# A pipelined attention kernel: a tail's first norm and what leads to it moved three steps ahead, beside the end of the tail before

## The reference, cut to what matters

```python
# x: (4, 1024, 256), 16 heads of 64, all float32
q, k, v = (einsum('bsd,hde->bhse', x, W) for W in (Wq, Wk, Wv))
attn = softmax(where(causal, q @ k.T / 8, -inf))
y = x + concat_heads(attn @ v) @ Wo
y = (y - mean(y)) * rsqrt(var(y) + 1e-3) * gamma + beta   # first norm
x1 = layernorm(x + y)                                     # second norm
h = silu(x1 @ wg.T) * (x1 @ wu.T)                         # hidden 768, int weights / 127
out = layernorm(x1 + h @ wd.T)                            # third norm
```

## Time and profile before

| what | value |
|---|---|
| median of three runs | 1456.25 us |
| the profiled execution, its own time | 1458.17 us |
| its span, first to last instruction | 1456.4 us |
| PE busy | 1409.0 us (97%) |
| DVE, ACT, POOL busy | 1031.7, 1002.1, 984.9 us (71, 69, 68%) |
| mean granted clock of TensorE | 0.991 |

### The profile page before, as it was taken

The page is one execution under the profiler, slowest core; times in us unless marked ns, Lnnn a source line. Parts: engine busy times, 40 slices in busy tenths (PEclk is TensorE's granted clock), DMA queues, the critical chain, the costliest instruction groups (busy, mean ns, idle before and its releaser), DMA issues.

```text
span 1456.4 us, 23825 instructions
## 1 busy us (share of the span) xinstructions
PE 1409.0 (97%) x7976; PEld 1231.7 (85%) x7976; DVE 1031.7 (71%) x2747; ACT 1002.1 (69%) x1924; POOL 984.9 (68%) x926
## 2 busy tenths in 40 slices
PE   7899999999999999999999999999999999999876
PEld 6788888888888888888888888888888888888766
DVE  7777776767676766777667676776767677677864
ACT  4777777877676676867668676676767668676534
POOL 4665666556676775867768586775867768588744
PEclk9999999999999999999999999999999999999998
DMA  3323222323342132322243122132313223121000
GB/s 130 102 81 93 62 67 95 117 52 90 103 123 73 52 95 59 110 54 58 74 117 95 52 61 72 56 120 59 95 44 110 74 60 95 51 64 55 23 12 30
DMA packets 61241, 110.46 MB, mean 76 GB/s; under 512 B 16256, under 2 KB 41600, under 8 KB 61120
## 3 DMA queue, kind: packets, MB, share of 16 engines
q1 hardware_dynamic: 61120, 108.94, 25.2%
HBM read 60.95 MB, written 13.89 MB: 51 GB/s over the span
## 4 chain that ended last, share of the span: by engine, by line
PE 73%; ACT 11%; DVE 8%; POOL 4%; issue 3%; DMA 1%; SPq 0%; ACTq 0%; POOLq 0%
PE bank L798 22%; PE bank L771 15%; PE bank L671 8%; PE bank L747 8%; PE bank L734 7%; PE bank L696 5%; PE bank L833 5%; PE bank L845 3%; ACT probs_hi L987 2%; POOL probs_lo L1428 2%; ACT probs L984 2%; ACT y_tail L1023 1%; ACT Q L967 1%; POOL h_lo L1470 1%; ACT K L967 1%
## 5 line engine op out<-in xcount | busy, mean ns | idle before, releaser
L1428 POOL TENSOR_TENSOR probs_lo<-probs,probs_hi 128x512 fp32r<-128x512 f32 x576 | 747.6, 1305 | 415.1 <-ACT probs_hi L987 412.5
L984 ACT ACTIVATE probs<-bank 128x512 f32<-128x512 f32 x576 | 344.2, 598 | 299.6 <-DVE bank L1185 217.8
L771 PE MATMUL bank<-Q,K 128*128 128x512 f32 (+3 forms) x1536 | 385.9, 353 | 3.4 <-ACT probs_hi L987 2.6
L987 ACT ACTIVATE probs_hi<-bank 128x512 fp32r<-128x512 f32 x576 | 342.2, 594 | 0.0
L771 PEld LDWEIGHTS bank<-Q,K 128*128 128x128 f32 x1536 | 252.1, 190 | 33.6 <-ACT probs_hi L987 6.2
L747 PE MATMUL bank<-K,Q 128*128 128x512 f32 (+3 forms) x768 | 245.5, 362 | 3.9 <-DMA Q<-Q 3.3
L1169 DVE CUSTOM_DVE_ANT_0 bank<-bank,mask_keys_free 128x128 f32<-128x128 f32 (+3 forms) x512 | 243.2, 506 | 4.7 <-PE bank L747 4.2
L798 PE MATMUL bank<-probs_hi,VH 128*128 128x512 f32 (+3 forms) x768 | 232.6, 343 | 7.9 <-POOL probs_lo L1428 7.2
L798 PE MATMUL bank<-probs_lo,VH 128*128 128x512 f32 (+3 forms) x768 | 234.7, 346 | 0.0
L798 PE MATMUL bank<-probs_hi,VL 128*128 128x512 f32 (+3 forms) x768 | 234.7, 346 | 0.0
L1185 DVE TENSOR_TENSOR bank<-bank,mask_queries_free 128x256 f32<-128x256 f32 (+1 forms) x320 | 119.4, 373 | 129.4 <-PE bank L771 128.9
(11 more groups left out here) (173 smaller groups left out, 2230.9 us busy)
## 6 DMA issues: line engine op xcount, KB each, us to landing
Q<-Q SPq DMA_DIRECT2D x64, 256.0 KB, 3.7
K<-K SPq DMA_DIRECT2D x64, 256.0 KB, 3.6
recip_bc<-recip_scratch SPq DMA_DIRECT2D x62, 256.0 KB, 3.4
wh<-w_scratch SPq DMA_DIRECT2D x12, 768.0 KB, 4.3
wl<-w_scratch SPq DMA_DIRECT2D x12, 768.0 KB, 5.8
wo_quad<-wo SPq DMA_DIRECT2D x16, 256.0 KB, 2.9
y<-x SPq DMA_DIRECT2D x16, 256.0 KB, 3.8
x_tail<-x SPq DMA_DIRECT2D x13, 256.0 KB, 4.4
```

Source lines behind the costliest of these rows:

```text
L771: last = mm(bk[:, at:at + cols], KX[:, n, P * i:P * i + P], QX[:, n, q0:q0 + cols], start=(KX is K1 and at == 0), stop=(KX is K2 and at + ...
L984: A(pe_[:, g % 2, :], stb[g % 2][:, :], ACT.Exp).then_inc(exp_done, 1)
L987: A(ph[:, g % RING, :], stb[g % 2][:, :], ACT.Exp).then_inc(hi_done, 1)
L1428: G.tensor_tensor(pl[:, g % RING, :], pe_[:, g % 2, :], ph[:, g % RING, :].bitcast(F32), ALU.subtract).then_inc(lo_done, 1)
```

## The change

The front of a tail, from its load to ADD, is due three steps earlier (N1, LN1R, GAM and ADD two steps earlier) for tails 0 to 10. LN2 and all that follows keep their steps, and so does the twelfth tail. Since the front now lies between the parts of the tail before, its parts count on semaphores of their own.

| part | LOAD | XB | LN1 | LN1R | N1 | GAM | ADD |
|---|---|---|---|---|---|---|---|
| engine | SP | POOL | DVE | POOL | ACT | POOL | POOL |
| step before | -5 | -1 | -1 | 0 | 1 | 2 | 3 |
| step after | -8 | -4 | -4 | -2 | -1 | 0 | 1 |

```diff
+EARLY = dict(LOAD=-8, XB=-4, LN1=-4, LN1R=-2, N1=-1, GAM=0, ADD=1)
-STEADY = tail_at(-5, -1, 7, [9, 23, 29], [13, 26, 32], 36)
-LAST_A = dict(tail_at(-5, -1, 7, [9, 18, 22], [12, 21, 25], 30), LN3=27, LN3R=28, OUT=29)
+STEADY = dict(tail_at(-5, -1, 7, [9, 23, 29], [13, 26, 32], 36), **EARLY)
+LAST_A = dict(tail_at(-5, -1, 7, [9, 18, 22], [12, 21, 25], 30), LN3=27, LN3R=28, OUT=29, **EARLY)
...
+        front_dve, front_pool = [sem(f"front_dve{g}") for g in range(2)], [sem(f"front_pool{g}") for g in range(2)]
+        front_act = [sem(f"front_act{g}") for g in range(2)]
...
-        DV = numbered(["st1a", "st1b", "mv1a", "mv1b", "st2a", "st2b", "mv2a", "mv2b", "x1lo"]
+        FRONT_DV = numbered(["st1a", "st1b", "mv1a", "mv1b"])
+        FRONT_PL = numbered(["xb", "e1", "r1", "m1", "s1", "gam", "add"])
+        FRONT_AC = numbered(["n1a", "n1b"])
+        FD, FP, FA = len(FRONT_DV), len(FRONT_PL), len(FRONT_AC)
+        DV = numbered(["st2a", "st2b", "mv2a", "mv2b", "x1lo"]
...
                 if g == 0 and tt:
-                    sp.wait_ge(tpool[0], NP * (tt - 1) + PL["add"])
+                    sp.wait_ge(front_pool[0], FP * tt)
...
             def t_ln2(n, g):
-                dve.wait_ge(tpool[g], NP * n + PL["add"])
+                dve.wait_ge(front_pool[g], FP * n + FRONT_PL["add"])
...
             def t_gamma(n, g):
-                pool.wait_ge(tact[g], NA * n + AC["n1b"])
-                G.tensor_tensor(rows_of(n, g), rows_of(n, g), over_rows(gm), ALU.mult).then_inc(tpool[g], 1)
+                pool.wait_ge(front_act[g], FA * n + FRONT_AC["n1b"])
+                G.tensor_tensor(rows_of(n, g), rows_of(n, g), over_rows(gm), ALU.mult).then_inc(front_pool[g], 1)
...
```

More of the change, by code:

```diff
@@ L311, in numbered @@
             return {k: n + 1 for n, k in enumerate(keys)}
-        DV = numbered(["st1a", "st1b", "mv1a", "mv1b", "st2a", "st2b", "mv2a", "mv2b", "x1lo"]
+        FRONT_DV = numbered(["st1a", "st1b", "mv1a", "mv1b"])
[3 more added lines that the diff above has]
+        DV = numbered(["st2a", "st2b", "mv2a", "mv2b", "x1lo"]
                       + [f"{k}{r}" for r in range(3) for k in ("tg", "hh", "h", "y2")] + ["st3a", "st3b", "mv3a", "mv3b"])
-        PL = numbered(["xb", "e1", "r1", "m1", "s1", "gam", "add", "e2", "r2", "m2", "s2", "hl0", "hl1", "hl2",
+        PL = numbered(["e2", "r2", "m2", "s2", "hl0", "hl1", "hl2",
                        "e3", "r3", "m3", "s3"])
-        AC = numbered(["n1a", "n1b", "n2a", "n2b", "x1hi", "tanh0", "tanh1", "tanh2", "n3a", "n3b"])
+        AC = numbered(["n2a", "n2b", "x1hi", "tanh0", "tanh1", "tanh2", "n3a", "n3b"])
         PEC = numbered(["tr", "g0", "u0", "d0", "g1", "u1", "d1", "g2", "u2", "d2"])
@@ L505, in tail_load @@
                 if g == 0 and tt:
-                    sp.wait_ge(tpool[0], NP * (tt - 1) + PL["add"])
+                    sp.wait_ge(front_pool[0], FP * tt)
                 if g == EXTRA:
                     sp.wait_ge(out_stored, 16 * (XTRA - 1))
-                    sp.wait_ge(tpool[0], NP * (XTRA - 1) + PL["add"])
+                    sp.wait_ge(front_pool[0], FP * XTRA)
                 j = tt % NQ
@@ L525, in f_load @@
                 elif j == 3:
-                    sp.wait_ge(tpool[EXTRA], PL["add"])
+                    sp.wait_ge(front_pool[EXTRA], FRONT_PL["add"])
                 sp.dma_start(F[j].xt, x_rows(NIT - NQ + j)).then_inc(f_loaded[j], 16)
@@ L1017, in copy_out, with t_norm1 @@
                     A(rsum[0:1, cols], pvb[c][0:1, :], ACT.Copy).then_inc(ht_copied, 1)
+            def t_norm1(n, g):
+                act.wait_ge(front_pool[g], FP * n + FRONT_PL["s1"])
+                x2 = rows_of(n, g)
+                for t in range(2):
+                    A(x2[:, t, :], x2[:, t, :], ACT.Identity, bias=stat(n, g).nb[:, t:t + 1], scale=stat(n, g).rs[:, t:t + 1]).then_inc(front_act[g], 1)
             def t_norm(n, key, g):
@@ L1091, in step @@
                     if ts == at["N1"]:
-                        t_norm(n, 1, gset)
+                        t_norm1(n, gset)
                     if ts == at["X2"]:
@@ L1232, in t_ln1 @@
                 dve.wait_ge(tail_loaded[g], 32 * (n + 1))
-                stats(n, rows_of(n, g), 1, g)
+                for t in range(2):
+                    V.bn_stats(stat(n, g).st[:, t, :], rows_of(n, g)[:, t, :]).then_inc(front_dve[g], 1)
+                dve.wait_ge(front_dve[g], FD * n + FRONT_DV["st1b"])
+                V.memset(carrier[:, :], 0.0)
+                for t in range(2):
+                    V.bn_aggr(stat(n, g).mv[:, t, :], stat(n, g).st[:, t, :]).then_inc(front_dve[g], 1)
             def t_ln2(n, g):
-                dve.wait_ge(tpool[g], NP * n + PL["add"])
+                dve.wait_ge(front_pool[g], FP * n + FRONT_PL["add"])
                 stats(n, rows_of(n, g), 2, g)
@@ L1440, in one, with front_own, rstd1, rstd @@
                 return ap.rearrange("p t o -> p (t o)")
-            def rstd(n, eps, r, g):
+            def front_own(n, key, g):
+                pool.wait_ge(front_pool[g], FP * n + FRONT_PL[key])
+            def rstd1(n, g):
+                pool.wait_ge(front_dve[g], FD * n + FRONT_DV["mv1b"])
+                G.tensor_tensor(stat(n, g).rs, one(stat(n, g).mv[:, :, 1:2]), eps_attn[:, :], ALU.add).then_inc(front_pool[g], 1)
+                front_own(n, "e1", g)
+                G.tensor_tensor(stat(n, g).rs, stat(n, g).rs, halves[:, :], ALU.pow).then_inc(front_pool[g], 1)
+                G.tensor_tensor(stat(n, g).nb, one(stat(n, g).mv[:, :, 0:1]), ones_[:, :], ALU.mult).then_inc(front_pool[g], 1)
+                front_own(n, "m1", g)
+                G.tensor_tensor(stat(n, g).nb, stat(n, g).nb, stat(n, g).rs, ALU.mult).then_inc(front_pool[g], 1)
+            def rstd(n, r, g):
                 pool.wait_ge(tdve[g], ND * n + DV[f"mv{r}b"])
-                G.tensor_tensor(stat(n, g).rs, one(stat(n, g).mv[:, :, 1:2]), eps[:, :], ALU.add).then_inc(tpool[g], 1)
+                G.tensor_tensor(stat(n, g).rs, one(stat(n, g).mv[:, :, 1:2]), eps_ln[:, :], ALU.add).then_inc(tpool[g], 1)
                 own(n, f"e{r}", g)
@@ L1457, in t_xb @@
                 pool.wait_ge(consts_loaded, 32)
-                G.tensor_tensor(T[g].xt, T[g].xt, over_rows(bt), ALU.add).then_inc(tpool[g], 1)
+                G.tensor_tensor(T[g].xt, T[g].xt, over_rows(bt), ALU.add).then_inc(front_pool[g], 1)
             def t_gamma(n, g):
-                pool.wait_ge(tact[g], NA * n + AC["n1b"])
-                G.tensor_tensor(rows_of(n, g), rows_of(n, g), over_rows(gm), ALU.mult).then_inc(tpool[g], 1)
+                pool.wait_ge(front_act[g], FA * n + FRONT_AC["n1b"])
+                G.tensor_tensor(rows_of(n, g), rows_of(n, g), over_rows(gm), ALU.mult).then_inc(front_pool[g], 1)
             def t_add(n, g):
-                own(n, "gam", g)
-                G.tensor_tensor(rows_of(n, g), rows_of(n, g), T[g].xt, ALU.add).then_inc(tpool[g], 1)
+                front_own(n, "gam", g)
+                G.tensor_tensor(rows_of(n, g), rows_of(n, g), T[g].xt, ALU.add).then_inc(front_pool[g], 1)
             def t_hl(n, r, g):
@@ L1498, in step @@
                     if ts == at["LN1R"]:
-                        rstd(n, eps_attn, 1, gset)
+                        rstd1(n, gset)
                     if ts == at["GAM"]:
@@ L1504, in step @@
                     if ts == at["LN2R"]:
-                        rstd(n, eps_ln, 2, gset)
+                        rstd(n, 2, gset)
                     if ts in at["HL"]:
@@ L1508, in step @@
                     if ts == at["LN3R"]:
-                        rstd(n, eps_ln, 3, gset)
+                        rstd(n, 3, gset)
                 for j, _ in finals(g, "R1"):
```

## The result

The changed kernel takes 1460.29 us (median of 13 runs, 1459.2 to 1461.52), the kernel before 1457.42 us (13 runs, 1454.54 to 1459.19). The ratio is 1.0022 with a 95% interval of [1.0014, 1.0029]: by this ratio it is slower by 3.2 us, between 2.0 and 4.2 (the two medians differ by 2.9). The forecast was a change of +4.3 us.

The account below looks back on a forecast made before the run. PE, busy 97% of the span, was taken as the bound; per boundary 1.28 us lost less 0.82 repaid, over ten 4.6, less 0.25 at the first, gives +4.3 us: 1460.5 against the median of 1456.25, range 1455.5 to 1465.5.

Parts of the forecast that it names:

- ten boundaries of +0.46: Boundaries 5/6 to 14/15, taken as alike: PE loses 1.28 us, regains 0.82 at step 4, net +0.46 each.
- one of -0.25: Boundary 4 to 5, without an old tail: N1 fills ACT's slip before the second Q copy, gaining 0.25 us.
- The first pause: PE at step 32's `pv(32)`: XB ahead of `probs_lo(32)` on POOL makes it 0.58 us late.
- both together: PE's lag from the pauses at `pv(32)` and `pv(34)`, 0.58 and 0.71 us, put at 1.28 us.
- the old pause: PE at step 4: `pv(2)` waits 0.82 us for `probs_lo(2)`, which waits for ACT; forecast to vanish.
- Saving 0: ACT's stretch: N1 costs about 1.0 us at either place, so `probs_hi(2)` still ends at 866.83.
- N1's 0.4 us to spare: ACT behind OUT: LN1R is done at 857.5 and N1 due at 857.94, so N1 does not wait.
- the tightest: ACT's input from PE with least margin: the second K copy, behind `probs_hi(2)`, so the stretch stands despite 1.28 us lag.
- The first rival: Only XB's 0.58 us pause comes and step 4 pays it back whole: 1456.0 us, chance 0.17.
- The second rival: ACT's stretch moves with PE, step 4's pause stays beside the new ones: +12.8 us, 1469, chance 0.08.

Follow-up runs that it names:

- e6: The kernel before with only a tail's two loads moved, to -8 instead of -5, and the separate semaphores; ratio 1.0002.
- e1: The changed kernel with XB alone put back to step 35 (-1) and counted behind LN1R; ratio 1.0004.
- e5: As e4, but with N1 at -1, inside ACT's unbroken stretch, instead of -5; ratio 1.0007.
- e4: The changed kernel with LN1 at -7, LN1R at -6, N1 at -5 and XB, GAM, ADD at 0, 1, 2; ratio 0.9942.
- e2: The changed kernel with N1, GAM and ADD put back to their old steps 1, 2, 3; ratio 1.0076.
- e3: The kernel before with only the loads at -8 and XB at -4, nothing else early; ratio 1.0021.

## Why the prediction was right

**The sum.** Forecast were ten boundaries of +0.46 and one of -0.25. The trace has ten that add 3.78 us together (877.45 - 873.67), 0.38 each, and a first one of -0.40; the second profile of the changed kernel has 3.87 and -0.05. At the first boundary `probs_hi(2)` ends 0.23 us earlier in both, as forecast (0.25), but the rest of that iteration varies by more than this from trace to trace (e6, which leaves N1 alone, has +0.33). The forecast of 4.6 was 0.8 us too large, which is most of the distance between +4.3 and the measured +3.2.

**POOL.** The order was as written down: 1.25 us for XB, and 1.34 for LN1R where 1.36 was taken. That XB is the one that tips it is shown by e1: without it, the four operations of LN1R leave `pv(34)` just free of a pause. It starts 0.10 to 0.13 us after the end of its `probs_lo` there, where 0.05 us is the distance in the paused ones.

**PE.** The first pause measured 0.49 us (forecast 0.58) and both together 1.19 (forecast 1.28; its two parts, 0.58 and 0.71, add up to 1.29). The term that was mis-sized is the distance from the end of `probs_lo` to the first matmul: 0.15 us was taken from step 4, and at steps 34 and 0 it is 0.05 (849.76 + 1.29, then 851.10). The matmul behind each late one slipped too, some 0.1 us each time, which the sum left out, so that step 1 starts 1.32 us late. That this is near the 1.28 forecast is luck: pauses taken 0.1 us too long stand against slips taken as nothing.

**What is paid back.** `pv(2)` is 0.48 us later than before, against a forecast of 0.46. The sum left out that the old pause also made the matmul behind it slip. The timeline of PE before the change, and after it:

```profile
868.65 0.45 PE L798 MATMUL bank<-probs_lo,VH 128*128 128x384 f32 x2
```

```profile
867.80 0.45 PE L806 MATMUL bank<-probs_lo,VH 128*128 128x384 f32 x2
```

This pair stood 0.31 us behind the start at 868.34, and stands 0.23 us behind the one at 867.57 now. With that 0.08 us the net is 0.38 to 0.40. At the boundary from 5 to 6 the net is only 0.12. `probs_hi(2)` came 0.27 us later there before the change, and I took all ten as alike.

**ACT.** "Saving 0" was right: 13.67 us for the stretch, against 13.57, and N1's 0.4 us to spare were there (0.42). e5 against e4 confirms the reason: inside the stretch N1's place does not matter, outside it is worth 0.93 us for each boundary.

**Where the reasoning was too short.** The text said that ACT's stretch stands because its inputs from PE are early enough, and named the second K copy as the tightest. It was the second Q copy. In the changed kernel it has no room at all: it starts at 859.94, 0.04 us after the last matmul of PE's projection:

```profile
859.51 0.39 PE L679 MATMUL bank<-xh,wl 128*128 128x512 f32 x1
```

The same 0.04 us stand between the two in e2 and e3, where the profile shows the copy waiting. It also starts 0.55 us after the `probs_hi` ahead of it, where it was 0.47 in the timeline of ACT before (859.65 to 860.12). So the copy is already held up by PE, by less than 0.1 us, for which the timeline shows no bracket, and this is most of the 0.10 us by which the stretch grew. The delay costs nothing, as `probs_lo(2)` ends 0.52 us ahead of `pv(2)` at 867.57. Without N1 ahead of it the copy would have come 1.0 us earlier and waited as in e2. The first rival, in which one pause of 0.58 us would be paid back whole, took for granted that the stretch stands; e3 shows that with N1 behind the Q copies it does not, and 0.3 us of the lag stay. N1's move was costed at nothing, and by itself it is; beside XB and LN1R it is worth 0.7 us for each boundary (e2 against the changed kernel, 88.32 and 87.63). The second rival, +12.8 us with the pause of step 4 beside the new ones, is in mechanism what e2 shows, at +11 us. What kept the forecast from turning into this rival is N1's new place ahead of the Q copies. The prediction did not name it as the reason, so that part of the result is luck. (A slip without effect: the range's upper end, 1465.5, lies three fifths and not two thirds of the way from 1460.5 to 1469.)

**DVE, SP, semaphores, clock.** All free, as forecast: LN1 in the wait of DVE, e6 at 1.0002, and the granted clock at 1.00 through both new pauses. The windows of the changed kernel are those of the length of one iteration, which holds one pause of each kind, and of ACT's stretch:

```profile
855.48:943.11 87.63, 86.67 (x498) 76.32 (x497) 60.73 (x169) 61.55 (x119) 62.21 (x59) 1.00 0.23 68
852.00:865.70 13.70, 13.27 (x70) 11.25 (x69) 9.18 (x24) 13.45 (x26) 11.46 (x16) 1.00 0.27 78
```

## What to carry to other kernels

Before moving work of an engine that is idle a third of the time, look for the stretches in which it is not: there every instruction put ahead delays all behind it by its whole cost, while an instruction moved within the stretch that sets the end gains nothing by itself. A lag of the bounding engine is paid back only if the queue that it would then have waited for does not itself wait for that engine; check the producer of each instruction in that queue, with its margin in the new order. Work belongs in the waits that a timeline shows in brackets, and the first and last instance of a pattern have other ones than the steady ones.

## What the runs showed of the hardware that was not expected

From the end of `probs_lo` on POOL to the start of the first matmul that needs it, 0.05 us passed at steps 34 and 0 of the changed kernel and 0.14 to 0.15 us at step 4 of the kernel before. Both repeat at all ten boundaries. What makes the difference was not tried.
